# Decoder layer on one core: where the weights' maximum is taken, which banks the latent queries use, when a feed-forward half runs, and the last tile in two halves

## The chip, the cores and the metric

The kernel runs on one core of one Trainium2 chip. The metric is the device time of one execution in microseconds (us), as a median over runs. Its engines are TensorE (PE in the profile, with PEld for its weight loads), VectorE (DVE), ScalarE (ACT), GpSimd (POOL) and SyncE (SP), which here only issues DMAs. The engines run their own instruction streams in order and meet through semaphores.

## The reference

Two batches of x (512 x 1024) pass through three steps, each followed by `layernorm(x + step(x))`:

```
attn : q = x@w_q (32 heads of 128), k, v = x@w_k, x@w_v (8 kv heads)
       lq = x@w_lq (256 wide);  lk = lq@w_lk, lv = x@w_lv (32 heads)
       rope on q, k, lk;  two causal attentions: (q,k,v) and (q,lk,lv)
       result = attn@w_o + lat@w_lo
cross: fake_quant(x) @ fake_quant(ctx)                  (512x1024 @ 1024x1024)
ffn  : x_scale = 448/max|x|, w_scale = 448/max|weight|
       clip(x*x_scale) @ clip(weight*w_scale) / (x_scale*w_scale)
```

`max|x|` and `max|weight|` are over the whole array, both batches for x.

## The kernel before

**Products.** Each fp32 operand is split into a high part (fp32r) and a low part, the difference; `product` (L1201) issues three matmuls, hi·hi, hi·lo, lo·hi. One product is 3 matmuls with 512 columns.

**The stream of weights.** Attention weights come in chunks of 128 x 512. SP loads a chunk into one of 4 slots (`load`, L289), ACT makes its high part (`high`, L470) four chunks ahead of use, POOL subtracts to get its low part (`low`, L410), TensorE waits for `lo_done` (`split`, L1277). A load waits for the low part that last used its slot, so POOL's order also paces SP. A batch has 4 chunks for the latent queries (LQ), then 8 groups (one kv head, four q heads and their latent heads) of 38 chunks, then a tail of 8 chunks of output weights.

**Banks.** PSUM has BANK_A 0 to 3 and BANK_B 0 to 3. BANK_A takes latent queries, latent keys, queries and output products; BANK_B takes k and v, latent values, scores, transposed probabilities (0 to 2) and attention outputs (3). Output products are added to `acc` by DVE (`add_part`, L834, semaphore `added`).

**Border of the batches.** TensorE ends batch 0 with the tail (`last_output`, L1453; `values` of the last unit is put ahead of chunk 2 of the tail, L1487), then runs the LQ products of batch 1, waits for `lq_lo_done` (both tiles), and for the column sums of the quantised ctx (`column_sums`, L1301), and starts group 0. The latent queries go bank, ACT copy (`lq_hi`, L688), DVE difference (`lq_lo`, L1044). In the first group of a batch the eight "previous output" chunks carry no work.

**The weights' maximum.** In batch 0 DVE takes the largest absolute value of each piece of the feed-forward weights (two pieces in each group, the second behind unit 1 of the attention, L986). POOL combines the 128 partitions by `partition_all_reduce` (L442) behind the low part of chunk 6 in the first group of batch 1. DVE needs the result (`w_all`) in the same group before it clips the weights.

**After the attention of batch 1.** TensorE's order is written out (L1545 to 1583): the tail's last four chunks with `transpose_x2` between, then feed-forward halves `ffn(tile, half)` (8 products into one bank), `transpose_q1` and `cross_product` of the late tiles. ACT's order is written out too; the part at issue is

```
            park(0)
            copy_q1T(TT)
            centre_q1(TT + 1)
            add_sums(TT + 1)
            shift_x1(TT + 3)
            copy_q1T(TT + 1)
            centre_q1(TT + 2)
```

where `centre_q1(i)` makes the `q` that `transpose_q1(i)` reads, and `copy_q1T(i)` copies that transpose out of its bank. For the last tiles `finish` (L1122) adds the product to the tile, takes the statistics of its two halves and combines them; ACT takes the root, `layernorm` (L1077) normalises, and SP stores 512 KB.

Of the kernel before, what the change touches and what calls it, by code (L numbers as in the profile page):

```python
# [14 lines left out]
P = 128  # L15
# [80 lines left out]
def program(nc, wstream, xt, x, ctxt, wf, cos, sin, mask, ident, quant, out):  # L96
    ctx = ExitStack()
    with ctx:
# [189 lines left out]
        def _(sp):  # L288
# [113 lines left out]
            for i in range(NT):  # L402
                sp.wait_ge(y_done, i + 1)
                sp.dma_start(out[i // TT, i % TT], tile(i)).then_inc(y_out, 16)
            sp.wait_ge(y_out, 16 * NT)
# [3 lines left out]
        def _(pool):  # L409
# [25 lines left out]
            def group(b, g, first):  # L435
                G = g + KVH * b
                for c in range(CHUNKS):
                    low(b, g, c, c)
                    if c == 6 and first and b:

                        pool.wait_ge(w_run_done, 2 * KVH)
                        nc.gpsimd.partition_all_reduce(col(W_ALL), col(W_RUN), P, RMAX).then_inc(w_all, 1)  # L442
                    if c == 12 and first:
                        wait(pool, colsum_ready, 2 * b)
                        nc.gpsimd.memset(col_part[:], 0.0).then_inc(cols_added, 1)
                    if c in (16, 28):
                        add_columns(b, G, (16, 28).index(c))
                    if b and first and C_PREV <= c < C_PREV + TT:
                        add_corr(c - C_PREV, corr0)
                    if b and c in (17, 33):  # L450
                        piece_low(2 * g + (17, 33).index(c))

            for b in range(B):
                for c in range(C_LQ):
                    low(b, 0, c - C_LQ, LQ_POS + c)
                group(b, 0, True)
                with pool.Fori(1, KVH) as g:
                    group(b, g, False)
                for c in range(C_TAIL):
                    low(b, KVH, c, TAIL_POS + c)  # L460
# [8 lines left out]
        def _(act):  # L469
# [206 lines left out]
            for b in range(B):  # L676
# [9 lines left out]
                for l in range(2):  # L686
                    act.wait_ge(*((chunk_used, chunk(b, 0, 0)) if l else (lq_ready, b + 1)))
                    nc.scalar.activation(lq_hi[:, l], BANK_A[l][:], ACT.Copy).then_inc(lq_hi_done, 1)  # L688
# [93 lines left out]
        def _(dve):  # L782
# [234 lines left out]
            for b in range(B):  # L1017
# [24 lines left out]
                for l in range(2):  # L1042
                    dve.wait_ge(lq_hi_done, 2 * b + l + 1)
                    nc.vector.tensor_tensor(lq_lo[:, l], BANK_A[l][:], lq_hi[:, l].bitcast(F32),  # L1044
# [77 lines left out]
            def finish(i):  # L1122
# [6 lines left out]
                dve.wait_ge(ffn_read, 2 * (i - TT) + 2)  # L1129
                moments_of(i, NT + i)  # L1130
# [63 lines left out]
            for i in range(TT + 1, NT):  # L1194
                finish(i)
                layernorm(i, NT + i, y_done)


        @block.tensor
        def _(pe):  # L1200
# [133 lines left out]
            def group(b, g, first):  # L1334
# [3 lines left out]
                for l in range(2):  # L1338
                    split(b, g, C_LK + l)
                    for h in range(HG):  # L1340
# [117 lines left out]
            for b in range(B):  # L1458

                for c in range(C_LQ):  # L1460
                    split(b, 0, c - C_LQ)
                    for k in (2 * c, 2 * c + 1):
                        if k % 2 == 0:

                            pe.wait_ge(x_lo_done, 4 * b + k // 2 + 1)
                        for l in range(2):
                            if k == 0 and b:

                                pe.wait_ge(added, 4 * (4 * KVH * b - 1) + l + 1)
                            at = LAT * (k % 2) + P * l  # L1470
                            last = product(BANK_A[l][:], weights(LQ_POS + c, at, at + P), xk(k),
                                           k == 0, k == KT - 1)
                            if k == KT - 1 and l == 0:
                                last.then_inc(lq_ready, 1)
                    last.then_inc(chunk_used, 1)

                pe.wait_ge(lq_lo_done, 2 * (b + 1))
# [8 lines left out]
                for i in range(C_TAIL // 2):  # L1486
                    if i == 2:  # L1487
# [68 lines left out]
            column_sums(1)  # L1556
            transpose_q1(TT)
            transpose_q1(TT + 1)
            ffn(1, 0)
# [88 lines left out]
```

## Time and profile before

| | |
|---|---|
| median of 3 runs | 2525.21 us (2523.72 to 2527.57) |
| the profiled execution | 2527.03 us, its span 2525.0 us |
| mean granted TensorE clock in it | 0.995 |
| PE busy | 2469.7 us, 98% of the span, 12456 matmuls |
| DVE, ACT, POOL busy | 1717.5 (68%), 1131.4 (45%), 922.4 us (37%) |
| chain of work that ended last | PE 94%, DVE 2%, ACT, issue, POOL and DMA 1% each |

The busy share tells which engine has work all the time. The chain follows the work back from the last instruction. The rows in the section below are of four kinds: the list of waits, the table of stretches with the granted clock (1.00 is 2.4 GHz, 0.50 is 1.2 GHz), the timeline, and the list of DMAs.

### The profile page before, as it was taken

The page shows a single profiled execution, that of the slowest core. Times are in us where ns is not written, and L with a number is a line of the kernel's source. Part 1 is how long each engine was busy: PE and PEld are TensorE (multiplying, and loading weights), DVE is VectorE, ACT ScalarE, POOL GpSimd, SP SyncE. Part 2 cuts the span into 40 slices and gives each one's busy share as a digit, 9 for nine tenths or more (in the row PEclk, how much of TensorE's full clock was granted, in tenths as well). Part 3 has the DMA queues.
Part 4 walks back from the last instruction along what each step waited for, and adds up shares of the span by engine and source line. Part 5 has one row for each costly group of instructions (what it writes and reads, how often), then busy time and mean ns, then how long its engine had stood idle before and what let it go on. Part 6 is the DMA issues. An engine that isn't in the chain of part 4 may idle for free.

```text
span 2525.0 us, 40729 instructions
## 1 busy us (share of the span) xinstructions
PE 2469.7 (98%) x12456; PEld 2088.6 (83%) x12456; DVE 1717.5 (68%) x3589; ACT 1131.4 (45%) x2576; POOL 922.4 (37%) x696
## 2 busy tenths in 40 slices
PE   8899999999999999999999999999999999999998
PEld 6688888888888888888767888888888888888877
DVE  5675767767676767666577676766767677667656
ACT  3444435344444434444364453544445353544551
POOL 4334242433434242433443425243342425334210
PEclk9999999999999999999999999999999999999999
DMA  5223231322323232323424323222232323234411
GB/s 180 88 80 92 63 102 58 96 61 70 93 75 96 59 102 60 89 66 97 127 90 134 105 71 106 69 85 77 83 104 71 106 73 106 61 92 145 154 34 67
DMA packets 124408, 226.26 MB, mean 90 GB/s; under 512 B 13089, under 2 KB 21409, under 8 KB 124193
## 3 DMA queue, kind: packets, MB, share of 16 engines
q1 hardware_dynamic: 119552, 216.91, 28.6%
q10 hardware_dynamic: 4768, 8.39, 1.0%
q8 instruction: 30, 0.49, 0.1%
q14 instruction: 58, 0.47, 0.1%
HBM read 206.37 MB, written 18.87 MB: 89 GB/s over the span
## 4 chain that ended last, share of the span: by engine, by line
PE 94%; DVE 2%; ACT 1%; issue 1%; POOL 1%; DMA 1%; SPq 0%; PEldq 0%; ACTq 0%; DVEq 0%; POOLq 0%
PE bank_a L1204 16%; PE bank_a L1206 16%; PE bank_a L1205 16%; PE bank_b L1204 13%; PE bank_b L1205 13%; PE bank_b L1206 13%; PE bank_b L1252 5%; PE bank_b L1521 1%; POOL w_lo L414 0%; DMA probs<-xt 0%; DVE probs L809 0%; ACT w_hi L478 0%; POOL acc L433 0%; PE bank_b L1388 0%; PE bank_a L1329 0%
## 5 line engine op out<-in xcount | busy, mean ns | idle before, releaser
L414 POOL TENSOR_TENSOR w_lo<-w_raw,w_hi 128x512 fp32r<-128x512 f32 x632 | 844.3, 1345 | 1413.9 <-ACT w_hi L478 1404.0
L478 ACT ACTIVATE w_hi<-w_raw 128x512 fp32r<-128x512 f32 x632 | 392.6, 626 | 291.8 <-DMA w_raw<-wstream 138.8
L1204 PE MATMUL bank_a<-w_hi,o_hi 128*128 128x512 f32 x1024 | 409.7, 400 | 4.2 <-issue 2.1
L1206 PE MATMUL bank_a<-w_hi,o_lo 128*128 128x512 f32 x1024 | 402.7, 393 | 0.0
L1205 PE MATMUL bank_a<-w_lo,o_hi 128*128 128x512 f32 x1024 | 402.1, 393 | 0.0
L515 ACT ACTIVATE probs<-probs,row_min 128x512 f32<-128x512 f32 (+3 forms) x512 | 281.7, 551 | 240.8 <-DVE row_min L809 238.5
L826 DVE TENSOR_TENSOR pT_lo<-bank_b,pT_hi 128x512 fp32r<-128x512 f32 (+1 forms) x384 | 207.0, 594 | 252.9 <-ACT pT_hi L521 252.9
L525 ACT ACTIVATE o_hi<-bank_b 128x512 fp32r<-128x512 f32 x128 | 76.8, 600 | 454.9 <-PE bank_b L1206 454.9
L820 DVE TENSOR_SCALAR probs<-probs,row_inv 128x512 f32<-128x512 f32 (+3 forms) x512 | 260.0, 567 | 4.5
L1204 PE MATMUL bank_a<-xT_hi,w_hi 128*128 128x512 f32 x544 | 216.3, 398 | 16.4 <-POOL w_lo L414 14.2
L1206 PEld LDWEIGHTS bank_a<-w_hi,o_lo 128*128 128x128 f32 x1024 | 192.6, 188 | 41.5
L1204 PEld LDWEIGHTS bank_a<-w_hi,o_hi 128*128 128x128 f32 x1024 | 193.0, 188 | 39.0 <-issue 2.6
L1205 PEld LDWEIGHTS bank_a<-w_lo,o_hi 128*128 128x128 f32 x1024 | 193.0, 189 | 34.8
L809 DVE CUSTOM_DVE_ANT_0 probs<-bank_b,mask_sb 128x512 f32<-128x512 f32 (+3 forms) x512 | 220.3, 482 | 1.4
L1205 PE MATMUL bank_a<-xT_lo,w_hi 128*128 128x512 f32 x544 | 214.3, 394 | 0.0
L1206 PE MATMUL bank_a<-xT_hi,w_lo 128*128 128x512 f32 x544 | 214.2, 394 | 0.0
L1204 PE MATMUL bank_b<-w_hi,xT_hi 128*128 128x512 f32 x512 | 199.2, 389 | 0.0
L1205 PE MATMUL bank_b<-w_lo,xT_hi 128*128 128x512 f32 x512 | 199.2, 389 | 0.0
L1206 PE MATMUL bank_b<-w_hi,xT_lo 128*128 128x512 f32 x512 | 199.2, 389 | 0.0
L521 ACT ACTIVATE pT_hi<-bank_b 128x512 fp32r<-128x512 f32 (+1 forms) x384 | 171.6, 518 | 18.0 <-PE bank_b L1252 18.0
L790 DVE TENSOR_TENSOR probs<-bank_a,cos_sb 128x512 f32<-128x512 f32 x128 | 88.2, 689 | 134.2 <-PE bank_a L1206 128.2
L1252 PE MATMUL bank_b<-ident_sb,probs 128*128 128x128 f32 x1280 | 162.4, 274 | 12.7 <-DVE row_min L809 12.3
(176 smaller groups left out, 4770.4 us busy)
## 6 DMA issues: line engine op xcount, KB each, us to landing
w_raw<-wstream SPq DMA_DIRECT2D x632, 256.0 KB, 2.7
stage<-ctx SPq DMA_DIRECT2D x32, 256.0 KB, 2.7
stage_w<-wf SPq DMA_DIRECT2D x32, 256.0 KB, 2.8
q_scratch<-stage_q SPq DMA_DIRECT2D x32, 128.0 KB, 1.7
wf_hi_scratch<-piece_hi SPq DMA_DIRECT2D x16, 256.0 KB, 3.1
wf_lo_scratch<-stage_w SPq DMA_DIRECT2D x16, 256.0 KB, 3.4
wf_hi<-wf_hi_scratch SPq DMA_DIRECT2D x8, 512.0 KB, 7.9
wf_lo<-wf_lo_scratch SPq DMA_DIRECT2D x8, 512.0 KB, 11.8
```

The costliest lines, as they stand in the source:

```text
L414: nc.gpsimd.tensor_tensor(w_lo[:, s], w_raw[:, r], w_hi[:, s].bitcast(F32), ALU.subtract).then_inc(lo_done, 1)
L478: nc.scalar.activation(w_hi[:, s], w_raw[:, r], ACT.Copy).then_inc(hi_done, 1)
L515: nc.scalar.activation(part, part, ACT.Exp, bias=row_min[:, u % 2, i:i + 1], scale=-1.0, accum_out=row_sum[:, u % 2, i:i + 1]).then_inc(ex ...
L521: nc.scalar.activation(pT_hi[:, at:at + w], BANK_B[bank][:, 0:w], ACT.Copy).then_inc(pT_hi_done, 1)
L790: nc.vector.tensor_tensor(a, bank[:], cos_sb[:], ALU.mult)
L809: nc.vector.tensor_tensor_reduce(out=probs[:, u % 2, at:at + w], in0=BANK_B[bank][:, col:col + w], in1=mask_sb[:, N - w:N], scale=-SCALE, ...
L820: nc.vector.tensor_scalar(part, part, row_inv[:, u % 2, i:i + 1], None, ALU.mult).then_inc(normed, 1)
L826: nc.vector.tensor_tensor(pT_lo[:, at:at + w], BANK_B[bank][:, 0:w], pT_hi[:, at:at + w].bitcast(F32), ALU.subtract).then_inc(pT_lo_done, 1)
L1204: nc.tensor.matmul(dst, still[0], move[0], start=start, stop=False)
L1205: nc.tensor.matmul(dst, still[0], move[1], start=False, stop=False)
L1206: return nc.tensor.matmul(dst, still[1], move[0], start=False, stop=stop)
L1252: last = nc.tensor.transpose(BANK_B[bank][:, dst:dst + P], probs[:, u % 2, src:src + P], ident_sb[:])
```

## The change

- POOL takes the all-reduce of the weights' maximum at the end of batch 0's groups, ahead of the low parts of the tail's eight chunks, and no longer in the first group of batch 1.
- The latent queries of both batches go to BANK_B 0 and 1. Their wait for `added` goes away. In the last LQ chunk both products of tile 0 come ahead of those of tile 1. The wait for `lq_lo` is taken per tile, ahead of the latent keys of the first group, and no longer ahead of the column sums.
- `values` of the last unit stands ahead of tail chunk 1, not 2, in both batches.
- `ffn(1, 0)` stands ahead of `transpose_q1(TT)`.
- `finish` takes each half's statistics right after that half's addition. The last tile is normalised and stored in two halves.

```diff
@@ SP
-            for i in range(NT):
+            for i in range(NT - 1):
                 sp.wait_ge(y_done, i + 1)
                 sp.dma_start(out[i // TT, i % TT], tile(i)).then_inc(y_out, 16)
-            sp.wait_ge(y_out, 16 * NT)
+            for half in range(2):
+                part = slice(N * half, N * (half + 1))
+                sp.wait_ge(y_done, NT + half)
+                sp.dma_start(out[B - 1, TT - 1, :, part], tile(NT - 1)[:, part]).then_inc(y_out, 16)
+            sp.wait_ge(y_out, 16 * (NT + 1))
@@ POOL, group
-                    if c == 6 and first and b:
-                        pool.wait_ge(w_run_done, 2 * KVH)
-                        nc.gpsimd.partition_all_reduce(col(W_ALL), col(W_RUN), P, RMAX).then_inc(w_all, 1)
@@ POOL, behind the groups
+                if b == 0:
+                    pool.wait_ge(w_run_done, 2 * KVH)
+                    nc.gpsimd.partition_all_reduce(col(W_ALL), col(W_RUN), P, RMAX).then_inc(w_all, 1)
                 for c in range(C_TAIL):
                     low(b, KVH, c, TAIL_POS + c)
@@ ACT (and DVE in the same way)
-                    nc.scalar.activation(lq_hi[:, l], BANK_A[l][:], ACT.Copy).then_inc(lq_hi_done, 1)
+                    nc.scalar.activation(lq_hi[:, l], BANK_B[l][:], ACT.Copy).then_inc(lq_hi_done, 1)
@@ DVE, finish
-                dve.wait_ge(ffn_read, 2 * (i - TT) + 2)
-                moments_of(i, NT + i)
+                    dve.wait_ge(ffn_read, 2 * (i - TT) + half + 1)
+                    link(nc.vector.bn_stats(stats[:, i, half], where))
+                nc.vector.bn_aggr(moments[:, i], stats[:, i].rearrange("p a n -> p (a n)")).then_inc(moments_ready, 1)
@@ DVE, last tile
-            for i in range(TT + 1, NT):
+            for i in range(TT + 1, NT - 1):
                 finish(i)
                 layernorm(i, NT + i, y_done)
+            i = NT - 1
+            finish(i)
+            dve.wait_ge(roots_ready, NT + i + 1)
+            link(nc.vector.reciprocal(spread[:, i:i + 1], spread[:, i:i + 1]))
+            for half in range(2):
+                where = tile(i)[:, N * half:N * (half + 1)]
+                nc.vector.tensor_scalar(where, where, moments[:, i, 0:1], spread[:, i:i + 1],
+                                        ALU.subtract, ALU.mult).then_inc(y_done, 1)
@@ PE, latent keys
                     split(b, g, C_LK + l)
+                    if first:
+                        pe.wait_ge(lq_lo_done, 2 * b + l + 1)
@@ PE, latent queries
-                    for k in (2 * c, 2 * c + 1):
-                        if k % 2 == 0:
-                            pe.wait_ge(x_lo_done, 4 * b + k // 2 + 1)
-                        for l in range(2):
-                            if k == 0 and b:
-                                pe.wait_ge(added, 4 * (4 * KVH * b - 1) + l + 1)
-                            at = LAT * (k % 2) + P * l
-                            last = product(BANK_A[l][:], weights(LQ_POS + c, at, at + P), xk(k),
-                                           k == 0, k == KT - 1)
+                    pe.wait_ge(x_lo_done, 4 * b + c + 1)
+                    pairs = [(k, l) for k in (2 * c, 2 * c + 1) for l in range(2)]
+                    for k, l in sorted(pairs, key=lambda a: a[1]) if c == C_LQ - 1 else pairs:
+                        at = LAT * (k % 2) + P * l
+                        last = product(BANK_B[l][:], weights(LQ_POS + c, at, at + P), xk(k), k == 0, k == KT - 1)
-                pe.wait_ge(lq_lo_done, 2 * (b + 1))
@@ PE, tail
-                    if i == 2:
+                    if i == 1:
                         values(KVH * (b + 1) - 1, UNITS - 1)
@@ PE, after the attention
             column_sums(1)
+            ffn(1, 0)
             transpose_q1(TT)
             transpose_q1(TT + 1)
-            ffn(1, 0)
             cross_product(0)
```

## Rows read from the trace of the kernel before

**Rows 1.** The page's engines: busy us, share of the span, instructions.
```profile
PE 2469.7 (98%) x12456; PEld 2088.6 (83%) x12456; DVE 1717.5 (68%) x3589; ACT 1131.4 (45%) x2576; POOL 922.4 (37%) x696
```

**Rows 2.** Waits of PE, whole span: us in total, times, longest.
```profile
PE bank_a L1204 <- POOL w_lo L414: 14.2, 2, 11.2
...
PE bank_a L1204 <- DVE acc L845: 2.2, 1, 2.2
PE bank_b L1316 <- ACT q L567: 2.2, 1, 2.2
...
PE bank_b L1305 <- DVE lq_lo L1044: 1.4, 1, 1.4
```

**Rows 3.** Stretches: length, PE busy (x matmuls), granted clock, DMA share, GB/s.
```profile
1199.50:1203.50 4.00, 3.29 (x8) 0.57 0.73 186
...
1237.50:1244.50 7.00, 6.19 (x15) 0.51 0.56 150
2418.00:2430.00 12.00, 9.76 (x52) 1.00 0.00 0
```

**Rows 4.** Timeline, start of batch 0: start, us, engine, line, operation [idle before].
```profile
23.73 1.28 ACT L688 ACTIVATE lq_hi<-bank_a 128x512 fp32r<-128x512 f32 x2 [2.50 <-PE bank_a L1206]
...
25.78 0.50 PE L1204 MATMUL bank_a<-lq_hi,w_hi 128*128 128x512 f32 x1 [1.41 <-DVE lq_lo L1044]
```

**Rows 5.** Timeline, latent queries of batch 1.
```profile
1200.21 0.77 PE L1204 MATMUL bank_a<-xT_hi,w_hi 128*128 128x512 f32 x1 [2.25 <-DVE acc L845]
...
1212.85 1.37 DVE L1044 TENSOR_TENSOR lq_lo<-bank_a,lq_hi 128x512 fp32r<-128x512 f32 x2 [7.75 <-ACT lq_hi L688]
...
1214.28 1.12 PE L1305 MATMUL bank_b<-col_part,ones 128*128 128x512 f32 x2 [1.41 <-DVE lq_lo L1044]
```

**Rows 6.** Timeline of POOL, 1145 to 1240 us.
```profile
1147.71 1.29 POOL L414 TENSOR_TENSOR w_lo<-w_raw,w_hi 128x512 fp32r<-128x512 f32 x1 [0.97 <-ACT w_hi L478]
...
1182.81 1.29 POOL L414 TENSOR_TENSOR w_lo<-w_raw,w_hi 128x512 fp32r<-128x512 f32 x1 [12.95 <-ACT w_hi L478]
...
1219.83 1.29 POOL L414 TENSOR_TENSOR w_lo<-w_raw,w_hi 128x512 fp32r<-128x512 f32 x1 [3.24 <-ACT w_hi L478]
1228.04 0.38 POOL L442 PARTITION_ALL_REDUCE sc<-sc  x1 [6.92 <-issue]
1237.00 3.73 POOL L414 TENSOR_TENSOR w_lo<-w_raw,w_hi 128x512 fp32r<-128x512 f32 x3 [8.58 <-issue]
```

**Rows 7.** Timeline of PE, first chunk of batch 0's tail.
```profile
1173.97 0.50 PE L1204 MATMUL bank_a<-w_hi,o_hi 128*128 128x512 f32 x1 [1.00 <-DVE o_lo L831]
```

**Rows 8.** Timeline of DVE, x of batch 1, third and fourth pair.
```profile
1194.76 1.23 DVE L992 TENSOR_TENSOR xT_lo<-probs,xT_hi 128x1024 fp32r<-128x1024 f32 x1
1197.41 2.06 DVE L992 TENSOR_TENSOR xT_lo<-probs,xT_hi 128x1024 fp32r<-128x1024 f32 x1 [1.43 <-ACT xT_hi L504]
```

**Rows 9.** Timeline of PE, transposes of x2 behind the tail of batch 1.
```profile
2393.66 0.55 PE L1504 MATMUL bank_b<-ident_sb,xs 128*128 128x128 f32 x3 [0.49 <-ACT xs L708]
```

**Rows 10.** Timelines of ACT and PE, 2418 to 2433 us.
```profile
2420.59 1.02 ACT L586 ACTIVATE q1T<-bank_b 128x1024 bf16<-128x1024 bf16 x1 [0.65 <-PE bank_b L1316]
...
2427.23 0.19 ACT L567 ACTIVATION_READ_ACCUMULATOR q<-q1f,sc 128x1 f32 x1
...
2422.79 0.62 PE L1316 MATMUL bank_b<-ident_b,q 128*128 128x128 bf16 x8 [2.24 <-ACT q L567]
2423.22 0.48 PE L1204 MATMUL bank_a<-wf_hi,x2T_hi 128*128 128x512 f32 x1
...
2428.79 3.63 PE L1521 MATMUL bank_b<-q,q1T 128*128 128x512 bf16 x16
2432.25 0.61 PE L1316 MATMUL bank_b<-ident_b,q 128*128 128x128 bf16 x8
```

**Rows 11.** The end: timeline of DVE; DMAs issued (KB, us to landing).
```profile
2518.92 1.42 DVE L1074 BATCH_NORM_STATS2 stats<-acc 128x6 f32<-128x512 f32 x2
...
out<-acc SPq DMA_DIRECT2D x2, 512.0 KB, 2.6
```

More of the change, by code:

```diff
@@ L1043, in _ @@
                     dve.wait_ge(lq_hi_done, 2 * b + l + 1)
-                    nc.vector.tensor_tensor(lq_lo[:, l], BANK_A[l][:], lq_hi[:, l].bitcast(F32),
+                    nc.vector.tensor_tensor(lq_lo[:, l], BANK_B[l][:], lq_hi[:, l].bitcast(F32),
                                             ALU.subtract).then_inc(lq_lo_done, 1)
@@ L1461, in _ @@
                     split(b, 0, c - C_LQ)
-                    for k in (2 * c, 2 * c + 1):
-                        if k % 2 == 0:
-                            pe.wait_ge(x_lo_done, 4 * b + k // 2 + 1)
-                        for l in range(2):
-                            if k == 0 and b:
-                                pe.wait_ge(added, 4 * (4 * KVH * b - 1) + l + 1)
-                            at = LAT * (k % 2) + P * l
-                            last = product(BANK_A[l][:], weights(LQ_POS + c, at, at + P), xk(k),
-                                           k == 0, k == KT - 1)
-                            if k == KT - 1 and l == 0:
-                                last.then_inc(lq_ready, 1)
+                    pe.wait_ge(x_lo_done, 4 * b + c + 1)
[3 more added lines that the diff above has]
+                        last = product(BANK_B[l][:], weights(LQ_POS + c, at, at + P), xk(k), k == 0, k == KT - 1)
+                        if k == KT - 1 and l == 0:
+                            last.then_inc(lq_ready, 1)
                     last.then_inc(chunk_used, 1)
-                pe.wait_ge(lq_lo_done, 2 * (b + 1))
                 if b:
```

## The prediction

> **What bounds the kernel.** I read the page's table of engines first: TensorE is busy for 98% of the span [rows 1], so a microsecond is won only where TensorE stands still, or runs slowly, or where nothing follows it at the very end. The list of TensorE's waits over the whole span comes next [rows 2]: there are few, and the change can reach 3.0 us of the wait for GpSimd's low parts (two waits, 14.2 in total, the longer of 11.2 at the start being out of reach), the wait of 2.2 for `acc`, that of 2.2 for `q`, and two of 1.4 for `lq_lo`. The third view is the table of stretches with the granted clock [rows 3]: around 1200 us and around 1238 us the clock stands at its lower level (1.2 of 2.4 GHz) for most of the stretch. Both begin with a TensorE wait, so those two waits cost more than their length. The timelines say what each wait is for.
>
> **Latent queries in the other banks, batch 0.** The key products of the first group waited for both `lq_lo` tiles, 1.41 us [rows 4]. Now the last chunk is ordered by tile: tile 0 is ready six matmuls before the end instead of three. A matmul costs 0.23 us (a feed-forward half of 24 goes from 2423.22 to 2428.79, 5.57 [rows 10]), so it comes 0.7 us earlier, and products with tile 0 wait for tile 0 alone. From its last product to `lq_lo` 0 it is an ACT copy and a DVE subtraction, half of the pairs' 1.28 [rows 4] and 1.37 [rows 5], or 1.3 us, against 6 x 0.23 = 1.4. What stays is under 0.1; tile 1 has twelve matmuls, 2.8 us, more. Gain 1.35 (1.2 to 1.4).
>
> **The same, batch 1: the bank.** The first product waited 2.25 us until DVE had added the last output product out of bank_a 0 [rows 5]. In bank_b 0 and 1 that wait is gone: their last readers, the low parts of the last probabilities, ran before the last `values`, which stands ahead in TensorE's order. What the products need else: `x_lo_done` of the first pair (DVE's third xT_lo started at 1194.76 [rows 8], so the first two are long done) and the last quarter at 1199.47, needed for the fourth chunk some 8 us after the start. Gain 2.25. The clock: of the 4.0 us from 1199.5 the mean grant is 0.57, so 4.0 x 0.43 = 1.7 us of full-speed work is lost, 0.1 of it while TensorE still stood. Gain 1.6 (0 to 1.7, if another wait took its place).
>
> **The same, batch 1: the column sums.** They waited 1.41 us for `lq_lo`, with which they have nothing to do [rows 5]. Without that wait the column sums (the first two matmuls alone 1.12) run in this gap, and the key products behind them need `lq_lo` 0 only, done about when the column sums begin, by the 1.3 and 1.4 us above. `lq_lo` 1 follows some 1.3 us behind the last product, far ahead of the second key chunk. Gain 1.4. `added` for all of bank_a is now asked for before the column sums, 10 us after it is true: nothing.
>
> **The weights' maximum.** On GpSimd the all-reduce itself is 0.38 us, but idle "issue" time of 6.92 stands before it and 8.58 after it: from the end of one low part at 1221.12 to the next at 1237.00 the queue loses 15.9 us [rows 6]. The low parts are four chunks ahead, about 11 us, so TensorE ran dry: 3.0 us [rows 2] plus the clock. From 1237.5 on, 7.0 us at a mean of 0.51 lose 3.4, of which 0.4 lies in the wait: 3.0. Removing it gains 6.0. In its new place it starts after the low part that ends at 1149.00. Behind it wait the low parts of the tail's first four chunks, SP's loads of the next four (each waits for a low part four back), and ACT's copies of those. With 15.9 the first tail low part ends at 1149.0 + 15.9 + 1.3 = 1166.2; TensorE reaches that chunk at 1172.97 (its products start at 1173.97 after a wait of 1.00 for `o_lo`) [rows 7]. Slack 6.8 us, so it costs nothing up to a swap of 22.7. The load for the fifth tail chunk goes out at 1166 and its low part was made at 1182.81 [rows 6]: 16 us for a transfer. What `W_RUN` needs is complete: the largest-weight step is in the middle of the group. Cost 0, low end 0, high end 1 us for this reason: the delayed low parts come closer to DVE's last normalisation, and `o_lo` behind it is what TensorE waits for. DVE's xT_lo took 1.23 us with GpSimd at rest, 2.06 with it busy [rows 8]. The Trainium skill ("GPSIMD Engine Reference", 1. Specifications) states the cause, SBUF interfaces shared with VectorE when an instruction has two SBUF inputs or uses both ports. By that rule each of the four normalising instructions could be held up, which would give up to four times 0.83 us, 3.3 in all; but after the swap four low parts end at 1164.9 + 4 x 1.3 = 1170, four microseconds before the products start, so I stay at 0.
>
> **`values` one chunk earlier.** In batch 0 nothing: DVE's addition behind the fourth chunk still paces the x tiles. In batch 1 ACT gets `o_hi` a chunk (2.7 us) earlier, so the second normalised tile of xs, which held the transposes for 0.49 [rows 9], is there before them. Gain 0.5. What could be late next is the raw chunk of the tail behind the many loads; it had no wait shown, and I give it 0 to 0.5.
>
> **The feed-forward half ahead of the transposes.** This doesn't do what it seems to. The 2.24 us at 2422.79 [rows 10] is the second transpose waiting for ACT's `q`; but ACT makes this `q` only after copying the first transpose out (2420.59), in its own order, which the diff leaves alone. So with 5.57 us of products ahead of the *first* transpose, ACT waits too, and the 2.24 comes behind them unchanged. Worse, those products no longer stand between the second and the third transpose. The third's `q` is read out at 2427.23 + 0.19 = 2427.42, 4.63 behind the start of the second transposes; now only the set of transposes (2422.79 to 2423.22) and 16 cross products (2428.79 to 2432.25) lie between, 0.43 + 3.46 = 3.89. The difference of 0.74 and a few hundredths until the semaphore is seen make 0.8 us of a new wait. Loss 0.8 (0 to 1.5).
>
> **The last tile by halves.** Statistics of the first half move ahead of the last product: of 1.42 us for two, half leaves the end [rows 11]. The normalisation in two pieces covers the same elements and costs one start more, under 0.1. The last transfer is half as large and starts at the same point; 512 KB take 2.6 from issue to landing [rows 11], much of it fixed: 0.3 (0 to 0.9). Gain 1.0 (0.6 to 1.6).
>
> **Sum.** 1.35 + 2.25 + 1.6 + 1.4 + 3.0 + 3.0 + 0.5 - 0.8 + 1.0 = 13.3 us. The profiled execution took 2527.03 (span 2525.0 and 2.0 around it): 2513.7. It is 1.8 above the median of the runs, 2525.21; if that offset is noise, the median comes to 2511.9; if it is one more slow stretch of the clock than usual, which the change now removes, to 2513.7. I take 2513.
>
> **Rivals.**
> 1. *The feed-forward step works*: both waits are hidden, 2.24 + 0.8 better: 2510. It needs ACT to make the second `q` before copying; its queue has the other order.
> 2. *The clock strikes elsewhere.* A wait of 2.25 at 1200 brought the lower level, one of 2.24 at 2422 did not (1.00) [rows 3]. The same wait at another moment can go either way: 1.6 more, also in the first group of batch 0: 2515 to 2516. The Trainium skill ("TensorE: Matmul & The Clock Gate", Part 1) calls the observation of activity free-running, so that the transition varies from run to run; the two rows agree.
> 3. *The gain at the border is given back*: in the first group of batch 1 ACT also quantises and corrects x, and if its chain rather than TensorE sets the pace there, the 6.0 us of GpSimd's stall come back as waits at 1284 to 1345: 2519. Against it: SP, ACT and DVE were held by the same stall and moved with TensorE.
> 4. *The swap is not hidden in its new place* (the slower side): beyond 22.7 us TensorE waits at the first tail chunk for each microsecond more. It undoes the change at 22.7 + 13.3 = 36 us, and is slower by 0.2% from 41 us on. It measures 15.9, with two large transfers beside it that the new place doesn't have. At 45 us it would be 2513 + 22 = 2535.
>
> **Chances.** Forecast 0.60, rival 1 0.06, rival 2 0.19, rival 3 0.09, rival 4 0.02, something else 0.04. The range 2508 to 2518 holds the first three cases with the bounds of the terms. The three runs of before lie within 0.15%, so 0.2% (5 us, 2520.2) is about what can be told from no change: faster 0.93, same 0.05, slower 0.02.
>
> **What would show it.** TensorE's wait for w_lo near 1238, for `acc` near 1200 and both for `lq_lo` gone, with full clock there; GpSimd idle "issue" on either side of the all-reduce near 1149 to 1165 and no TensorE wait behind it; near 2414 a wait of 2.2 for `q` behind the feed-forward half, and a second of 0.8; one bn_stats after the last product. I'd be wrong if the `q` wait is gone, if waits near 1270 to 1335 grow, or if the first tail chunk waits for w_lo.

## The result, and the profile after

The changed kernel takes 2514.48 us (median of 5 runs, 2513.51 to 2514.78) against 2526.14 for the kernel before on the same chip (5 runs, 2523.72 to 2529.17): ratio 0.9949, 95% interval 0.9938 to 0.9961. The forecast was 2513, range 2508 to 2518, faster. The profiled execution took 2514.78 us with a span of 2512.8, so 12.2 us less than before by either figure; the sum in the prediction, which started from that execution, said 13.3. By the medians it is 11.7 us.

The list of TensorE's waits, whole span, of the changed kernel (us in total, times, longest), against [rows 2]:

```profile
PE bank_b L1218 <- POOL w_lo L419: 13.3, 2, 11.2
...
PE bank_b L1330 <- ACT q L572: 2.9, 2, 2.2
...
PE bank_a L1218 <- DVE lq_lo L1049: 0.4, 1, 0.4
```

Of the 13.3 for `w_lo`, 11.2 is the start and 2.1 a wait in the first scores of batch 0 that the kernel before has too (in another row, as its latent queries were in the other banks); the 3.0 at the border is gone. The wait for `acc` and that of the column sums are gone, `lq_lo` is down from 1.4 to 0.4 in batch 0, and the wait for `q` has *grown*, from one to two. The stretches with the granted clock (length, PE busy and matmuls, clock, DMA share, GB/s), against [rows 3]:

```profile
87.50:91.00 3.50, 3.37 (x11) 0.52 0.27 75
1198.00:1210.00 12.00, 12.00 (x53) 1.00 0.65 193
1231.00:1245.00 14.00, 14.00 (x65) 1.00 0.34 119
```

The border runs at full clock (2.4 GHz) without a gap. But near 87 us there is a stretch at the lower level (1.2 GHz), right behind a wait. The kernel before shows none behind the same wait:

```profile
87.00:91.00 4.00, 2.14 (x12) 1.00 0.35 124
```

(This last line is of the kernel before, where the wait ends at 88.5.) Both kernels wait 2.08 us there.

Timelines of the changed kernel: DVE and PE at the start of batch 0 [rows 4]; PE at the border [rows 5]; POOL around the all-reduce in its new place [rows 6].

```profile
22.67 1.02 DVE L1043 TENSOR_TENSOR sc<-sc 128x1 f32<-128x1 f32 x1
23.73 0.16 DVE L1044 TENSOR_TENSOR sc<-sc 128x1 f32<-128x1 f32 x1
23.92 0.16 DVE L1045 TENSOR_TENSOR sc<-sc 128x1 f32<-128x1 f32 x1
24.12 0.69 DVE L1049 TENSOR_TENSOR lq_lo<-bank_b,lq_hi 128x512 fp32r<-128x512 f32 x1
24.96 0.47 PE L1218 MATMUL bank_a<-lq_hi,w_hi 128*128 128x512 f32 x1 [0.38 <-DVE lq_lo L1049]
...
1198.21 0.39 PE L1218 MATMUL bank_b<-xT_hi,w_hi 128*128 128x512 f32 x1
...
1209.10 1.88 PE L1319 MATMUL bank_b<-col_part,ones 128*128 128x512 f32 x4
1210.41 0.80 PE L1218 MATMUL bank_a<-lq_hi,w_hi 128*128 128x512 f32 x1
```

```profile
1148.11 1.29 POOL L419 TENSOR_TENSOR w_lo<-w_raw,w_hi 128x512 fp32r<-128x512 f32 x1 [0.95 <-ACT w_hi L483]
1156.02 0.38 POOL L463 PARTITION_ALL_REDUCE sc<-sc  x1 [6.62 <-issue]
1163.55 2.55 POOL L419 TENSOR_TENSOR w_lo<-w_raw,w_hi 128x512 fp32r<-128x512 f32 x2 [7.16 <-issue]
```

The two gaps of GpSimd around the all-reduce are still there, 14.15 us from low part to low part (this whole is called the swap below), and TensorE has no wait behind them. Late in the kernel, ACT and PE, against [rows 10]:

```profile
2413.85 1.02 ACT L591 ACTIVATE q1T<-bank_b 128x1024 bf16<-128x1024 bf16 x1 [6.13 <-PE bank_b L1330]
2414.77 1.14 ACT L572 ACTIVATE q<-q1f,sc 128x1024 bf16<-128x1024 f32 x1
...
2416.06 0.62 PE L1330 MATMUL bank_b<-ident_b,q 128*128 128x128 bf16 x8 [2.25 <-ACT q L572]
...
2420.74 0.62 PE L1330 MATMUL bank_b<-ident_b,q 128*128 128x128 bf16 x8 [0.61 <-ACT q L572]
```

ACT stands idle for 6.13 us behind the feed-forward half, then copies, then makes the `q` for which TensorE waits. The end [rows 11], DVE:

```profile
2507.60 0.69 DVE L1135 BATCH_NORM_STATS2 stats<-acc 128x6 f32<-128x512 f32 x1
...
2509.10 1.00 DVE L1209 TENSOR_SCALAR acc<-acc,moments,spread 128x512 f32<-128x512 f32 x2
```

**Where the 12.2 us came from.** TensorE runs nearly the same list of matmuls in both kernels, so the distance between the starts of the same two matmuls can be compared. Each number is a difference of two times in the timelines, of one profiled execution of each kernel.

| stretch of TensorE | before | after | change | predicted |
|---|---|---|---|---|
| first product to first latent keys, batch 0 | 14.58 | 13.75 | -0.83 | -1.35 |
| to the first tail chunk of batch 0 | 1148.19 | 1149.41 | +1.22 | 0 |
| tail to the LQ products of batch 1 | 26.24 | 23.84 | -2.40 | -2.25 |
| to the first keys of batch 1 | 15.49 | 12.20 | -3.29 | -3.0 (1.6 + 1.4) |
| to the transposes of v | 31.00 | 24.94 | -6.06 | -6.0 (3.0 + 3.0) |
| to the tail of batch 1 | 1132.19 | 1132.34 | +0.15 | 0 |
| tail to the second column sums | 39.33 | 38.29 | -1.04 | -0.5 |
| to `ffn(1, 1)` | 18.35 | 19.20 | +0.85 | +0.8 |
| to the end of the last matmul | 81.53 | 81.53 | 0 | 0 |
| from there to the end of the span | 6.94 | 6.09 | -0.85 | -1.0 |

### The profile page after: what moved, and what is told of

It is laid out like the page before. It is cut to its first block, busy times and chain, and to the rows that moved or that the text cites. A ratio compares the mean times of both kernels' runs of the same rounds, so it can differ in the third digit from the quotient of the medians.

```text
span 2512.8 us, 40738 instructions
## 1 busy us (share of the span) xinstructions
PE 2466.1 (98%) x12456; PEld 2087.0 (83%) x12456; DVE 1718.5 (68%) x3590; ACT 1134.5 (45%) x2576; POOL 921.6 (37%) x696
## 4 chain that ended last, share of the span: by engine, by line
PE 94%; DVE 2%; ACT 1%; issue 1%; POOL 1%; DMA 1%; SPq 0%; DVEq 0%; PEldq 0%; ACTq 0%; POOLq 0%
PE bank_a L1220 16%; PE bank_a L1219 16%; PE bank_a L1218 16%; PE bank_b L1218 13%; PE bank_b L1219 13%; PE bank_b L1220 13%; PE bank_b L1266 5%; PE bank_b L1531 0%; DMA probs<-xt 0%; POOL w_lo L419 0%; DVE probs L814 0%; ACT probs L520 0%; POOL acc L438 0%; PE bank_b L1404 0%; PE bank_b L1514 0%
## 5 line engine op out<-in xcount | busy, mean ns | idle before, releaser
L1218 PE MATMUL bank_a<-xT_hi,w_hi 128*128 128x512 f32 x512 | 200.5, 392 | 0.0
L1220 PE MATMUL bank_a<-xT_hi,w_lo 128*128 128x512 f32 x512 | 199.6, 390 | 0.0
L1219 PE MATMUL bank_a<-xT_lo,w_hi 128*128 128x512 f32 x512 | 199.5, 390 | 0.0
L1266 PE MATMUL bank_b<-ident_sb,probs 128*128 128x128 f32 x1280 | 162.1, 274 | 12.5 <-DVE row_min L814 12.2
```

Of the source, the lines that this page charges most:

```text
L1218: nc.tensor.matmul(dst, still[0], move[0], start=start, stop=False)
L1219: nc.tensor.matmul(dst, still[0], move[1], start=False, stop=False)
L1220: return nc.tensor.matmul(dst, still[1], move[0], start=False, stop=stop)
L1266: last = nc.tensor.transpose(BANK_B[bank][:, dst:dst + P], probs[:, u % 2, src:src + P], ident_sb[:])
```

## The experiments

Twelve kernels, in three groups; those of one group ran on the same chip with the kernel before. Ratios are to the kernel before, with 95% intervals. Medians of different groups, and those of the changed kernel, were taken at different times, so small differences between them say less than the stretches of the profiles do.

**First group: the late step and the weights' maximum.**

*ffn_back*, the changed kernel with

```
-            ffn(1, 0)
             transpose_q1(TT)
             transpose_q1(TT + 1)
+            ffn(1, 0)
```

> The changed kernel with one step undone: the feed-forward half stands behind the second late transpose again. My theory (the step moves the wait for q and adds one): one wait of 2.2 us for q at the second transpose, none at the third, so 0.6 us less waiting than the changed kernel (which shows 2.25 and 0.61), 0.6 us faster. Rival (the step helps): slower than the changed kernel by about 2 us, because the 2.2 is a wait that it had hidden.

Measured: 2512.07 us, 0.9943 [0.9929, 0.9956]. From the second column sums to `ffn(1, 1)` 18.35 us, as before the change (19.20 with it), with one wait:

```profile
2410.97 0.62 PE L1330 MATMUL bank_b<-ident_b,q 128*128 128x128 bf16 x8 [2.24 <-ACT q L572]
```

So the moved half costs 0.85 us; the rival falls. The median moved more (2.4), which is more than this step does in the profile; the two intervals overlap, and a stretch of lower clock can add or spare as much (below).

*act_order*, the changed kernel with

```
@@ ACT
             park(0)
-            copy_q1T(TT)
             centre_q1(TT + 1)
             add_sums(TT + 1)
             shift_x1(TT + 3)
-            copy_q1T(TT + 1)
+            copy_q1T(TT)
             centre_q1(TT + 2)
+            copy_q1T(TT + 1)
             add_sums(TT + 2)
@@ PE
-            ffn(1, 0)
             transpose_q1(TT)
+            ffn(1, 0)
             transpose_q1(TT + 1)
```

> The changed kernel with ACT's order altered too: the q of the second transpose is made before the first transpose is copied out, and TensorE runs transpose, feed-forward half, transpose. My theory (ACT's own order is what makes TensorE wait for q): both waits, 2.25 and 0.61 us, are gone and none over 0.3 takes their place, 2.9 us faster than the changed kernel, some 0.994 of the kernel before. Rival (ACT as a whole is too slow between 2405 and 2430): the waits come back at a later transpose or cross product, and the gain is under 1 us.

Measured: 2510.74 us, 0.9937 [0.9923, 0.9950]. The stretch is 15.93 us, 3.27 less than in the changed kernel and 2.42 less than before, and its list of waits is empty. By the medians it is 3.7 us faster than the changed kernel, where 2.9 were expected. ACT and PE:

```profile
2406.48 1.14 ACT L572 ACTIVATE q<-q1f,sc 128x1024 bf16<-128x1024 f32 x1
...
2410.26 1.00 ACT L591 ACTIVATE q1T<-bank_b 128x1024 bf16<-128x1024 bf16 x1
...
2412.55 0.62 PE L1330 MATMUL bank_b<-ident_b,q 128*128 128x128 bf16 x8
```

The `q` that was late by 2.25 us is made in ACT's gap of 6.13. The wait was ACT's order.

*max_only*, the kernel before with only the all-reduce moved:

```
@@ POOL, group
-                    if c == 6 and first and b:
-                        pool.wait_ge(w_run_done, 2 * KVH)
-                        nc.gpsimd.partition_all_reduce(col(W_ALL), col(W_RUN), P, RMAX).then_inc(w_all, 1)
@@ POOL, behind the groups
+                if b == 0:
+                    pool.wait_ge(w_run_done, 2 * KVH)
+                    nc.gpsimd.partition_all_reduce(col(W_ALL), col(W_RUN), P, RMAX).then_inc(w_all, 1)
```

> The kernel before with only the weights' maximum moved to the end of batch 0. My theory: the wait of 3.0 us for w_lo near 1238 and the lower clock behind it go, 6.0 us faster than the kernel before (ratio 0.9976); the swap of GpSimd's code in the new place costs no wait of TensorE. Rival (the gain is given back by ACT's and DVE's chain in the first group of batch 1): waits between 1284 and 1345 grow, and less than 3 us are won. Rival (the lower clock has another cause than this wait): it is still there near 1238, and 3.0 us are won.

Measured: 2520.60 us, 0.9975 [0.9966, 0.9984]. Keys to transposes of v: 24.93 us, as in the full change (24.94). From there on to a matmul 97 us later (1343.58 in the kernel before) it takes 97.03 us against 96.87 before: nothing is given back, so that rival falls too. Its clock (same columns as above):

```profile
1199.50:1203.50 4.00, 4.00 (x20) 1.00 0.62 194
2414.00:2417.40 3.40, 3.40 (x15) 0.50 0.00 0
```

The code around both stretches is that of the kernel before, yet the lower level behind the wait for `acc` (1.8 here) is absent, and one stands behind the wait for `q` of 2.24, where the kernel before had none. There the stretch to `ffn(1, 1)` took 19.95 instead of 18.35: 1.6 us.

*max_back*, the changed kernel with the same diff the other way round.

> The changed kernel with the weights' maximum back in the first group of batch 1, all else of the change kept. My theory (the terms add up): 6 us slower than the changed kernel, half of the whole gain, with a wait of some 3 us for w_lo and two stretches of lower clock behind it. Rival (the terms overlap: what the latent queries win at the border is lost again in this wait, because GpSimd's stall starts from a low part that does not move as far as TensorE does): the wait is longer than 3 us, up to 3 plus 5.3, and the kernel is up to 11 us slower than the changed one.

Measured: 2518.91 us, 0.9970 [0.9958, 0.9982], 4.4 slower than the changed kernel, where 6 was expected. Wait, and clock:

```profile
PE bank_a L1217 <- POOL w_lo L419: 3.1, 1, 3.1
```

```profile
1231.00:1238.00 7.00, 6.39 (x21) 0.76 0.55 152
```

Keys to transposes of v 29.98, so 5.04 more than the changed kernel: the wait is no longer than before, and only one stretch of lower clock stands behind it, not two as I had expected. The gains of the latent queries and of the maximum add up; they don't cover each other.

**Second group: the latent queries, the swap made longer, the store.**

*latent_only*, the kernel before with the latent queries' part of the change:

```
@@ ACT, and DVE in the same way
-                    nc.scalar.activation(lq_hi[:, l], BANK_A[l][:], ACT.Copy).then_inc(lq_hi_done, 1)
+                    nc.scalar.activation(lq_hi[:, l], BANK_B[l][:], ACT.Copy).then_inc(lq_hi_done, 1)
@@ PE, latent keys
+                    if first:
+                        pe.wait_ge(lq_lo_done, 2 * b + l + 1)
@@ PE, latent queries: the lines of the change, and
-                pe.wait_ge(lq_lo_done, 2 * (b + 1))
```

> The kernel before with only the latent queries' part of the change (other banks, order of the last chunk, waits per tile). My theory: at the border the wait for acc (2.25 us), that of the column sums for lq_lo (1.4) and, where it fell, the lower clock behind the first (1.6) go, and the wait for w_lo near 1238 stays at 3.0; in batch 0 some 1.0 us goes, of which a stretch of lower clock near 87 us can take 1.1 back. So 4.7 to 6.3 us faster than the kernel before. Rival (the latent queries gain nothing while GpSimd's stall stands behind them): the wait for w_lo grows to more than 6 us and under 2 us are won.

Measured: 2518.92 us, 0.9969 [0.9958, 0.9981]. Tail to LQ 23.85, LQ to keys 12.21, both as in the full change; keys to transposes 30.07, with a wait for `w_lo` of 3.2 and 0.9 less than before through one stretch of lower clock fewer. The rival falls. By the medians 7.1 us are won, more than the 4.7 to 6.3 expected; the two stretches give 5.7, that 0.9 and batch 0 (12.93 us to the first keys, against 14.58) the rest.

*swap_twice* and *swap_thrice*, the changed kernel with, behind the all-reduce, once or twice

```
+                    nc.gpsimd.tensor_tensor(col(W_PART), col(W_RUN), col(W_RUN), ALU.subtract)
+                    nc.gpsimd.partition_all_reduce(col(X_ALL), col(W_RUN), P, RMAX)
```

(the second time with two other columns; nobody reads the results).

> The changed kernel with a second all-reduce (of the same column, into one that is free then) behind the first, with a small subtraction between them, so that GpSimd goes through the swap twice, 28 us instead of 14. My theory (a slack of 22.7 us, then one for one): the first low part of the tail is ready about 1179 instead of 1165, TensorE waits some 5.6 us for it at the first tail chunk, 1 to 2 us more at the fifth, whose load goes out later by as much, and a stretch of lower clock may add 1.7 or 3.4: 7 to 11 us slower than the changed kernel. Rival (the small subtraction needs no swap, or two all-reduces in a row share one): no wait, no difference. Rival (the slack is larger, since ACT and SP have their own reserve): under 3 us.

> The changed kernel with three all-reduces, each behind a small subtraction: 42 us in the swap. My theory: the first tail chunk waits some 20 us for w_lo, 18.8 us more than the changed kernel lost there, and with a later wait and the clock it is 20 to 26 us slower than the changed kernel, so slower than the kernel before by 8 to 14 us. Rival (the delay is given back at the border, where SP's loads and DVE's additions would have been waited for anyway): under 15 us slower than the changed kernel.

Measured: 2519.80 us, 0.9976 [0.9965, 0.9987], and 2533.51 us, 1.0029 [1.0018, 1.0040]. POOL and PE of *swap_thrice*:

```profile
1146.40 1.29 POOL L419 TENSOR_TENSOR w_lo<-w_raw,w_hi 128x512 fp32r<-128x512 f32 x1 [0.97 <-ACT w_hi L487]
1154.00 0.38 POOL L463 PARTITION_ALL_REDUCE sc<-sc  x1 [6.32 <-issue]
1161.24 0.18 POOL L464 TENSOR_TENSOR sc<-sc 128x1 f32<-128x1 f32 x1 [6.87 <-issue]
...
1190.32 0.77 PE L1222 MATMUL bank_a<-w_hi,o_hi 128*128 128x512 f32 x1 [18.68 <-issue]
```

From low part to low part GpSimd loses 27.67 us with two and 41.28 with three; the stretch from a matmul near 120 us to the first tail chunk takes 1057.53 and 1071.17 us, where the twelve other profiles have 1053.5 (to within 0.15). That is 4.0 and 17.7 more: 13.64 between the two, for a swap 13.61 longer. So the slack is 27.67 - 4.03 = 23.6 us, and beyond it the delay counts one for one. Up to the LQ products 2.5 and 2.0 us come on top, where the lower clock follows the wait. My 22.7 was counted to where TensorE reached the chunk, before its own wait of 1.0: 23.7. The fifth tail chunk was waited for in neither, and here my expectation was wrong: by the medians the two kernels are 5.3 and 19.0 us slower than the changed one, below the 7 to 11 and 20 to 26 that I had said. The rivals fall all the same: the swap is paid each time, and the delay is not given back. *swap_thrice* is slower than the kernel before although everything else of the change is in it: that is the prediction's rival 4 at work, and by these figures (an estimate) the change is undone at a swap of about 23.6 + 12.2 - 2 = 34 us.

*store_whole*, the changed kernel with the last tile normalised and stored in one piece, `finish` as changed:

```
@@ SP
-            for i in range(NT - 1):
+            for i in range(NT):
                 sp.wait_ge(y_done, i + 1)
...
@@ DVE
-            for i in range(TT + 1, NT - 1):
+            for i in range(TT + 1, NT):
                 finish(i)
                 layernorm(i, NT + i, y_done)
```

> The changed kernel with the last tile normalised and stored whole, as before; the statistics by halves are kept. My theory: of the 0.8 us won at the end (from the last matmul to the end of the span) 0.7 is from the statistics and only 0.1 from the store by halves, so at most 0.2 us slower than the changed kernel. Rival (the shorter last transfer is what wins): 0.6 to 0.9 us slower, seen in the stretch from the last matmul's end to the end of the span.

Measured: 2514.87 us, 0.9953 [0.9940, 0.9967]. From the last matmul to the end it is 6.26 us, against 6.09 with halves and 6.94 before: 0.68 is from the statistics, 0.17 from the halves. The normalisation is 0.81 us whole and 1.00 in two; a transfer of 256 KB takes 2.1 from issue to landing, one of 512 KB 2.6.

**Third group.**

*act_order_alone*, *act_order* with

```
-            transpose_q1(TT)
             ffn(1, 0)
+            transpose_q1(TT)
             transpose_q1(TT + 1)
```

> The changed kernel with ACT's order altered as in the run act_order, but TensorE's order left as the change has it (feed-forward half, then both transposes). My theory (both orders matter): the waits for q are gone, but the first cross product now comes right behind the two transposes and waits for ACT's copy of the first, 0.7 to 1.3 us; 1.6 to 2.2 us faster than the changed kernel, about 1 slower than act_order. Rival (ACT's order is all): no wait in its place, equal to act_order within 0.3 in the stretch up to the third transpose.

Measured: 2509.98 us, 0.9935 [0.9921, 0.9948]. The stretch is 16.73 us, 0.80 more than *act_order*, with this wait:

```profile
2412.61 3.63 PE L1531 MATMUL bank_b<-q,q1T 128*128 128x512 bf16 x16 [0.67 <-ACT q1T L591]
```

ACT's order gives 2.47 of the 3.27 us, a little more than expected, and TensorE's the rest. The medians of the two kernels can't be told apart.

*banks_only*, the kernel before with `BANK_B` for `BANK_A` in ACT's, DVE's and PE's lines of the latent queries, and

```
-                            if k == 0 and b:
-                                pe.wait_ge(added, 4 * (4 * KVH * b - 1) + l + 1)
```

> The kernel before with the latent queries in the other two banks and no wait for added, the order of the last chunk and both waits for lq_lo as before. My theory: at the border the wait of 2.25 for acc goes with the lower clock behind it where that falls there, the column sums' wait of 1.4 and that of batch 0 stay; 2.3 to 3.9 us faster than the kernel before, and 1.4 us slower than latent_only between the start of the latent queries and the column sums. Rival (the banks are all that matters): the column sums' wait shrinks too, as ACT and DVE read a bank nobody else uses, and the two kernels are equal there.

Measured: 2523.50 us, 0.9985 [0.9976, 0.9994]. Tail to LQ 23.85 us (26.24 before), LQ to keys 13.87 (15.49 before, 12.21 in *latent_only*), so 1.66 lie in the order and the waits per tile; both waits of 1.4 for `lq_lo` are there. The wait for `w_lo` behind is 3.6 and its stretch 31.67, 0.67 more than before: this part alone gave a little back.

*values_back*, the changed kernel with

```
-                    if i == 1:
+                    if i == 2:
                         values(KVH * (b + 1) - 1, UNITS - 1)
```

> The changed kernel with the last unit's values ahead of the third tail chunk again. My theory: a wait of 0.5 us for xs at the transposes near 2382, nothing in batch 0: 0.5 us slower between the tail of batch 1 and those transposes, not to be told in the median. Rival (it costs more: ACT's o_hi stands before the normalised tiles and the tail's high parts, so two things come late): 1 us or more, with a wait for w_lo or o_lo in a tail chunk.

Measured: 2513.22 us, 0.9950 [0.9936, 0.9963]. Tail to LQ in batch 0 23.85 (23.84 with the change): nothing, as said. In batch 1 tail to column sums 39.39 against 38.29, 1.1 us:

```profile
2378.35 1.06 PE L1514 MATMUL bank_b<-ident_sb,xs 128*128 128x128 f32 x8
2379.91 0.77 PE L1514 MATMUL bank_b<-ident_sb,xs 128*128 128x128 f32 x5 [0.50 <-ACT xs L713]
```

No tail chunk waits, so the rival's cause isn't there, but its size is. The first tile of xs is late too: its transposes start 0.14 us behind the end of the products, where matmuls that wait for nothing start 0.16 before it. That 0.3 is too short for the list. The last 0.25 is the run of transposes broken in two (2.41 us from the first to the next product, with the wait of 0.5, against 1.66 unbroken).

*constants_later*, *act_order* with DVE's last seven constants (L1039 to L1045) moved:

```
@@ DVE, batch 0
-                    link(nc.vector.tensor_scalar(col(NRZ1), col(RZ1), -1.0, None, ALU.mult))
-                    ...
-                    nc.vector.tensor_tensor(col(C3), col(ND2), col(S12), ALU.mult).then_inc(scalars, 1)
                 for l in range(2):
                     dve.wait_ge(lq_hi_done, 2 * b + l + 1)
...
                     nc.vector.tensor_copy(ident_b[:], ident_sb[:]).then_inc(tables, 1)
+                    link(nc.vector.tensor_scalar(col(NRZ1), col(RZ1), -1.0, None, ALU.mult))
+                    ...
```

> The run act_order with one thing more: seven one-column operations of DVE (the constants of the quantisation) stand behind the latent queries' low parts in batch 0 instead of ahead of them. My theory (what was left of the wait for lq_lo in batch 0, 0.2 to 0.4 us, and the 2.58 that max_only showed, is DVE still at its constants): wait 0.1 to 0.2 in every run, up to 0.3 us faster than act_order, nothing in the median. Rival (the chain copy then subtraction is longer than the six matmuls): the wait stays at 0.2 to 0.4. Risk: the first rotation waits behind the constants, and more than that is lost at the first keys.

Measured: 2509.45 us, 0.9932 [0.9919, 0.9946], the lowest median of all; it isn't to be told from *act_order*. PE, then DVE:

```profile
24.79 0.47 PE L1218 MATMUL bank_a<-lq_hi,w_hi 128*128 128x512 f32 x1 [0.22 <-DVE lq_lo L1041]
```

```profile
23.95 0.69 DVE L1041 TENSOR_TENSOR lq_lo<-bank_b,lq_hi 128x512 fp32r<-128x512 f32 x1 [2.46 <-ACT lq_hi L693]
```

DVE now waits for ACT, and the 0.22 is the chain of copy and subtraction itself, as the rival says; it stands in six other profiles, *act_order* and *latent_only* among them. The risk did not come true: from the first keys to the wait near 87 us it is 62.66 us in both kernels. What the constants cost shows in other profiles. In *max_back* ACT's copy ended at 23.07 and DVE, at its constants until 23.73, began `lq_lo` at 23.76: a wait of 0.80, some 0.6 of it theirs. In *max_only* it is some 1.2 of a wait of 2.58. In *act_order_alone* and *values_back*, where TensorE ended its LQ products about a microsecond earlier, the wait was 1.3 and 1.4, but only some 0.2 of that is DVE; most of it is ACT, whose copy began late, behind two high parts of weights that had just landed (*act_order_alone*, ACT):

```profile
21.90 1.28 ACT L483 ACTIVATE w_hi<-w_raw 128x512 fp32r<-128x512 f32 x2 [3.12 <-DMA w_raw<-wstream]
23.08 1.07 ACT L693 ACTIVATE lq_hi<-bank_b 128x512 fp32r<-128x512 f32 x2
```

Elsewhere the copy begins 0.93 us ahead of the last LQ matmul, here 0.04 (23.12). Moving the constants can't take that part away, and no run shows how much of the rest it saves, as this run's LQ products ended late (24.57).

## Why the prediction was right, point by point

- **Border.** The three stretches there gave 11.75 us, predicted 11.25. *max_only*, *latent_only* and *banks_only* take them apart: the all-reduce 6.06 (predicted 6.0), the banks 2.4 and the clock behind the wait 1.6 (2.25 and 1.6), the order and the waits per tile 1.66 (1.4). Each of the two parts alone gives its share. The clock's share is the one that was not certain: *max_only* shows that the lower level can stay away behind the same wait, a little shorter.
- **GpSimd's new place.** No cost, with a slack measured at 23.6 (predicted 22.7) against a swap of 14.2. One reading on the way was wrong: I took the 16 us between the first and the fifth tail low part for a transfer. In *swap_twice* the fifth starts 8.8 us behind the end of the first, so most of it is not. In the kernel before, ACT made that chunk's high part only at 1182.11, in its order behind a copy of `o_hi` for which it had waited 7.87 us for TensorE. A second reading was loose: the xT_lo of 1.23 us [rows 8] did not run with GpSimd at rest, as GpSimd began a low part at 1195.32, in its middle (one with GpSimd idle, at 1188.14 in the changed kernel, took 1.22). Neither enters the sum.
- **Batch 0.** The term of 1.35 was too large. The wait fell by 1.03; 0.16 of what stays is DVE behind its constants, which the row of before couldn't show, since there `lq_lo` came after an idle DVE, and 0.22 the chain, which I had put under 0.1. The stretch from the first product gave 0.83, as the products themselves took 0.2 longer. What the term left out is what ACT and DVE have ahead of the copy and the subtraction in their own orders: in the eleven profiles with the new order the wait is 0.22 us seven times, here 0.38, and 0.80, 1.27 and 1.42 in the other three. So how much of the term comes out changes from execution to execution.
- **Values.** 0.5 predicted, 1.04 measured: I priced the one wait that the list shows, and *values_back* shows two costs beside it. The five profiles with the old place have 39.3 to 39.4 us in that stretch, the nine with the new one 38.2 to 38.3.
- **The feed-forward half.** A loss of 0.8 predicted, 0.85 measured, by the working given: the 2.2 stays and 0.6 is new; the other 0.24 is not taken apart by any run. This step of the change is a loss; *ffn_back* is better in this stretch by 0.85, *act_order* by 3.3.
- **The end.** 0.85 measured, 1.0 predicted; the statistics give 0.68 (predicted 0.7), normalising and storing by halves 0.17 where I said 0.3 less under 0.1, as the second start costs 0.19.
- **The clock.** Rival 2 came true in part, beside the forecast: the new stretch near 87 us. From the first scores of batch 0 to a matmul near 120 us the 14 profiles, all with the same wait of 2.08, take 31.2 to 33.1 us; four of them show the changed kernel's pattern, a short stretch of the lower level from that wait on and two more later (the changed kernel, *ffn_back*, *act_order*, *store_whole*), and are the slowest, 33.1 each. Others have a longer one from there on and take 31.2 (*max_only*, *swap_thrice*, *constants_later*); the wait for `row_min` behind it is 1.3 to 1.4 there and 3.0 to 3.3 in the rest. The kernel before took 32.0. So 1.1 us lies in where the clock fell; kernels whose code is the same up to that point (*act_order*, *values_back*, *swap_twice*, *swap_thrice*) show 33.1, 31.4, 32.3 and 31.2, so it isn't the edit. It is as large as the whole difference between 13.3 and 12.2, and that is luck: the misses of the other terms (0.5 too much in batch 0, 0.5 too little at the border, 0.5 too little for `values`, and smaller ones) nearly cancel.

## What to carry to other kernels

Before a block of work is moved in front of a wait, look up in the other engine's own order what stands ahead of the awaited result: if the first of those instructions needs the block's end, the wait only moves, and the cure is in that engine's order. The same look belongs to the price of a wait: a chain of copy and subtraction lasts as long as its two instructions only if nothing stands ahead of them. A stall that can't be removed (here 14 us of GpSimd for 0.4 us of work) goes where its consumer is furthest behind, and the slack there, the consumer's arrival less the producer's, can be tested by making the stall longer. The removal of a wait can give more than the list shows: for `values`, waits too short for the list and the restart of a broken run doubled it.

## What the runs showed of the hardware

**The same wait does not always bring the lower clock.** The wait of 2.24 or 2.25 us for `q` stands in 11 profiles; in four of them (*max_only*, *max_back*, *store_whole*, *swap_thrice*) the granted clock fell to 1.2 GHz behind it, in seven not. It cost 1.6 us with TensorE's order of before, and 0.8 with that of the change, where the wait of 0.61 behind it vanished in exchange. Waits of 3.0 to 3.6 for `w_lo` at the border brought it in four of four, that of 2.25 for `acc` in its one profile, one of 1.8 in *max_only* did not. Behind the wait of 2.08 near 87 us it came in seven of 14. In *swap_twice* it came near 1295 us behind waits of 1.8 and 0.9:

```profile
1295.00:1298.50 3.50, 3.00 (x7) 0.51 0.62 188
```

The Trainium skill ("TensorE: Matmul & The Clock Gate", Part 1) says that the observation of activity is free-running and that the transition varies for that reason; these profiles agree.

**Going to the all-reduce and coming back cost GpSimd about the same**, 5.8 to 6.9 us there and 6.7 to 7.5 back in the quiet place. The size of the ordinary operation makes no difference: a subtraction of one column takes 0.18 us and has the same gaps around it. At the border, beside two loads of 1 MB each, it was 6.5 to 6.6 and 9.1 to 9.5 in three more profiles, 16.0 to 16.5 in all, beside the 15.9 of [rows 6]. Two all-reduces with one small ordinary operation between them pay twice. That the loads are what makes the way back longer is not shown by a run of its own.

**A DVE operation on one column can take 0.16 or 1.2 us.** The timelines of DVE and of POOL of the changed kernel:

```profile
21.14 2.54 POOL L419 TENSOR_TENSOR w_lo<-w_raw,w_hi 128x512 fp32r<-128x512 f32 x2 [0.57 <-ACT w_hi L483]
21.19 1.25 DVE L1041 TENSOR_TENSOR sc<-sc 128x1 f32<-128x1 f32 x1
22.48 0.15 DVE L1042 TENSOR_SCALAR sc<-sc 128x1 f32<-128x1 f32 x1
```

While POOL subtracts (21.14 to 23.68), DVE's `TENSOR_TENSOR` ends only with POOL's instruction (1.25, and 1.02 from 22.67), while the `TENSOR_SCALAR` between them takes 0.15; once POOL is done, `TENSOR_TENSOR` takes 0.16 (23.73, above). The Trainium skill ("GPSIMD Engine Reference", 1. Specifications) names this case, two SBUF inputs on interfaces that both engines share; the rows agree. It is why a handful of constants took DVE up to the moment at which `lq_lo` was wanted. It goes the other way too: in the kernel before, the low part that GpSimd began at 1195.32, with DVE in the middle of its xT_lo (1194.76 to 1195.99), took 1.82 us where 1.29 is usual.
